# A vision block with tree feed-forward on one core: leaves of six trees gathered by indirect DMA instead of four

## The reference

```python
h = patches @ W.T + b                                # 768 -> 256
h = h + attn(layernorm(h))                           # gated attention, no softmax
h = h + ffn(layernorm(h))
# attn(x): xn = x / rms(x) * g;  u, v, base = split(silu(xn @ uv_w.T))   # 512, 512, 128
#   q, k = rope(base * gamma + beta);  kernel = relu((q k' + w_rel) / sqrt(128)) ** 2
#   return x * res_scale + (u * (kernel @ v)) @ o_w.T
# ffn(x): 8 trees of 255 nodes; logits = x @ W_in.T + b_in
#   from the root go right where logits > 0, seven times: 8 nodes visited per tree
#   return (silu(logits) * visited) @ W_out.T
```

## Time and profile before

| | |
|---|---|
| median of three runs | 2206.93 us |
| profiled execution | 2201.36 us, its span 2199.5 us |
| mean granted TensorE clock | 0.981 of 2.4 GHz |
| busy in the span: PE, VectorE, ScalarE, GpSimd | 94%, 74%, 63%, 35% |
| DMA queue of the indirect DMAs | 103.02 MB, 17.4% of the 16 engines |
| DMA queue of all others | 59.71 MB, 9.3% |

### The profile page before, as it was taken

How to read it: one execution, slowest core, us unless ns; L and a number is a source line. 1 busy time by engine, 2 the same in 40 slices (tenths; PEclk the granted TensorE clock), 3 DMA queues, 4 the chain that set the end, 5 groups by cost and what they waited for, 6 DMA issues and landing times.

```text
span 2199.5 us, 42461 instructions
## 1 busy us (share of the span) xinstructions
PE 2066.1 (94%) x13256; PEld 1941.8 (88%) x13256; DVE 1621.5 (74%) x4210; ACT 1395.2 (63%) x3085; POOL 774.1 (35%) x905
## 2 busy tenths in 40 slices
PE   6899999999999999999999999999999999999997
PEld 5789889899988898888998898988889988889887
DVE  5678777777777787777777777777777877777775
ACT  5556666666666566566666665666665666656654
POOL 2752333232333333332323333323323233333233
PEclk8999999999999999999999999999999999999999
DMA  5331322222322223222223222222223232222222
GB/s 146 85 94 52 89 73 66 73 76 63 83 71 65 81 55 84 75 64 73 77 62 84 70 73 73 64 75 77 65 70 84 55 85 69 73 73 66 63 67 74
DMA packets 81999, 163.13 MB, mean 74 GB/s; under 512 B 17102, under 2 KB 48048, under 8 KB 81968
## 3 DMA queue, kind: packets, MB, share of 16 engines
q0 software_dynamic: 40960, 103.02, 17.4%
q1 hardware_dynamic: 41008, 59.71, 9.3%
HBM read 148.76 MB, written 13.90 MB: 74 GB/s over the span
## 4 chain that ended last, share of the span: by engine, by line
PE 84%; another core or an unknown queue 5%; ACT 4%; POOL 3%; issue 2%; DVE 1%; DMA 1%; ACTq 0%; POOLq 0%; SPq 0%; DVEq 0%
PE front L1142 10%; PE front L1144 9%; PE front L1143 9%; PE hid_ps L1142 9%; PE hid_ps L1143 9%; PE hid_ps L1144 9%; PE out_acc L1142 6%; PE out_acc L1143 6%; PE out_acc L1144 6%; PE out_acc L1378 4%; PE front L1177 2%; PE front L1184 2%; PE hid_ps L1366 2%; PE hid_ps L1337 2%
## 5 line engine op out<-in xcount | busy, mean ns | idle before, releaser
L474 POOL DMA_INDIRECT leaf_rows<-leaf_table,leaf_at x512 | 532.4, 1040 | 163.9 <-issue 163.4
L453 POOL TENSOR_TENSOR inv_root<-to_root,minus_half 98x8 f32<-98x8 f32 x64 | 111.0, 1734 | 728.3 <-DVE to_root L885 404.6
L528 ACT ACTIVATE hid_hi<-hid 128x392 fp32r<-128x392 f32 (+1 forms) x256 | 177.8, 695 | 237.1 <-PE out_acc L1144 155.4
L1142 PE MATMUL out_acc<-hid_hi,outw_lo 128*128 128x392 f32 x768 | 293.4, 382 | 2.6 <-DVE hid_lo L835 2.3
L1142 PE MATMUL hid_ps<-ffn_x,in_lo 128*128 128x392 f32 x768 | 282.3, 368 | 6.2 <-POOL in_lo L445 5.8
L1143 PE MATMUL hid_ps<-ffn_x,in_hi 128*128 128x392 f32 x768 | 266.3, 347 | 0.0
L1144 PE MATMUL hid_ps<-ffn_x,in_hi 128*128 128x392 f32 x768 | 264.7, 345 | 0.0
L1144 PE MATMUL out_acc<-hid_hi,outw_hi 128*128 128x392 f32 x768 | 264.6, 345 | 0.0
L1143 PE MATMUL out_acc<-hid_lo,outw_hi 128*128 128x392 f32 x768 | 264.4, 344 | 0.0
L473 POOL TENSOR_TENSOR held<-minus_half 98x1 f32<-98x1 f32 x128 | 47.2, 369 | 489.9 <-issue 428.7
L718 ACT ACTIVATE leaf_rows<-leaf_rows,leaf_act 98x256 f32<-98x256 f32 x512 | 218.2, 508 | 0.1
(11 more groups left out here) (140 smaller groups left out, 5808.2 us busy)
## 6 DMA issues: line engine op xcount, KB each, us to landing
x_raw<-x SPq DMA_DIRECT2D x192, 196.0 KB, 2.4
out<-out_stage SPq DMA_DIRECT2D x32, 392.0 KB
leaf_rows<-leaf_table,leaf_at POOLq DMA_INDIRECT x512
leaf_table<-leaf_rows SPq DMA_DIRECT2D x4, 256.5 KB, 4.7
out_stage<-in_w SPq DMA_DIRECT2D x4, 256.0 KB
tok_major<-tok_w SPq DMA_DIRECT2D x3, 256.0 KB, 4.3
late_raw<-out_w SPq DMA_DIRECT2D x6, 128.0 KB
u<-uv_w SPq DMA_DIRECT2D x1, 576.0 KB, 4.2
```

Source lines behind the costliest of these rows:

```text
L453: pool.tensor_tensor(inv_root[:, 0:size], to_root[:, 0:size], minus_half[:, 0:size], ALU.pow).then_inc(roots_ok, 1)
L474: pool.indirect_dma_start(row_slot(s, g), None, table, bass.IndirectOffsetOnAxis(ap=leaf_at[:, s, g:g + 1], axis=0), element_offset=s * P ...
L528: act.activation(out, src, ACT.Copy).then_inc(done, 1)
L1142: pe.matmul(out, w[1], x_parts[0], start=start, stop=False)
```

## The change

Trees 0 to 5 are gathered and 6 and 7 dense; there are 12 row slots, so tree s takes the slots of tree s - 3. The slots of the hidden values get names but stay two. The rounds are cut elsewhere, and all five lists of calls are ordered anew. Core of the diff:

```diff
-GATHERED = 4
+GATHERED = 6
-ROW_SLOTS = 8
+HID_SLOTS, HID_HALVES = 2, 2
+ROW_SLOTS = 12
-LATE_SPLITS = (((0, 1), (2,), (3,), (4,), (5,)), ((6,), (7,), (8, 9), (10, 11), (12, 13)))
+LATE_SPLITS = (((0, 1), (2,), (3,), (4,), (5,)), ((6,), (7,), (8,), (9,), (10, 11)))
...
                     act.wait_ge(decided, TREES * i + t + 1)
-                if b == halves(t) - 1 and (t >= 2 or not first(i)):
-                    act.wait_ge(hid_lo_ok, TREES * i + t - 1)
+                if t >= HID_SLOTS or not first(i):
+                    act.wait_ge(hid_lo_ok, TREES * i + t - HID_SLOTS + 1)
```

More of the change, by code:

```diff
@@ L771, in body @@
                 silu_v(n, 2)
                 silu_v(n, 3)
-                v_high(n, 2)
[L774 to L783, removed]
+                x_high(nx, 2)
+                leaf_silu(i, 1)
+                qk_high(n, 0)
@@ L784, in body @@
+                leaf_number(i, 3)
+                silu_u(n, 0)
+                qk_high(n, 1)
+                scale_rows(i, 1)
+                silu_u(n, 1)
+                silu_tree(i, 5, 0)
+                leaf_silu(i, 2)
+                v_high(n, 2)
+                leaf_number(i, 4)
                 if first(n):
                     build_rows()
+                v_high(n, 3)
+                scale_rows(i, 2)
                 kern_high(n, 0)
+                hid_high(i, 4)
                 kern_high(n, 1)
@@ L1410, in body @@
-                mix(i, 2)
-                tree_visits(p, 6)
-                mix(i, 3)
-                tree_out(p, 3, 1)
-                tree_out(p, 4, 0)
-                project_o(i, 0, range(0, 3))
-                project_o(i, 0, range(3, EC))
-                project_o(i, 1, range(0, EC))
-                embed(n, 0)
-                turn_h(i, 1, 0)
-                turn_h(i, 1, 1)
-                tree_out(p, 4, 1)
-                embed(n, 1)
-                tree_logits(p, 7, 0)
-                tree_logits(p, 7, 1)
@@ new lines, in body @@
+                turn_normed(n, 0)
+                turn_normed(n, 1)
+                tree_visits(i, 3)
+                tree_out(i, 1, 0)
+                make_base(n)
+                find_leaf(i, 2)
+                tree_out(i, 1, 1)
+                make_v(n, 0)
+                make_v(n, 1)
+                tree_logits(i, 4, 0)
+                tree_logits(i, 5, 0)
+                make_v(n, 2)
+                tree_out(i, 2, 0)
+                tree_visits(i, 4)
+                find_leaf(i, 3)
@@ L1450, in body @@
+                tree_out(i, 2, 1)
+                make_v(n, 3)
+                add_rows(i, 0)
+                make_u(n, 0)
+                make_u(n, 1)
+                tree_logits(i, 6, 0)
+                tree_visits(i, 5)
+                find_leaf(i, 4)
+                scores(n, 0)
+                tree_out(i, 3, 0)
                 if first(n):
                     turn_rows()
-                tree_out(p, 7, 1)
-                tree_logits(i, 4, 0)
-                turn_xn(n, 0)
-                turn_xn(n, 1)
@@ L1471, in body @@
-                tree_out(i, 2, 0)
-                make_v(n, 3)
-                add_rows(i, 0)
-                tree_out(i, 2, 1)
+                tree_out(i, 3, 1)
+                scores(n, 1)
+                add_rows(i, 1)
+                tree_logits(i, 6, 1)
+                tree_logits(i, 7, 0)
+                find_leaf(i, 5)
+                make_u(n, 2)
+                make_u(n, 3)
+                add_rows(i, 2)
+                mix(n, 0)
+                tree_visits(i, 6)
+                mix(n, 1)
@@ new lines, in body @@
+                mix(n, 2)
+                mix(n, 3)
+                tree_logits(i, 7, 1)
+                tree_out(i, 4, 0)
+                tree_out(i, 4, 1)
+                project_o(n, 0, range(0, 3))
+                project_o(n, 0, range(3, EC))
+                project_o(n, 1, range(0, EC))
+                tree_out(i, 5, 0)
+                tree_out(i, 5, 1)
+                turn_h(n, 1, 0)
+                turn_h(n, 1, 1)
+                embed(nx, 0)
+                embed(nx, 1)
+                embed(nx, 2)
@@ new lines, in body @@
+                embed(nx, 3)
+                tree_visits(i, 7)
+                embed(nx, 4)
+                embed(nx, 5)
+                turn_ffn_x(n, 0)
+                turn_ffn_x(n, 1)
+                add_rows(i, 3)
+                add_rows(i, 4)
+                turn_h(nx, 0, 0)
+                turn_h(nx, 0, 1)
+                tree_logits(n, 0, 0)
+                tree_logits(n, 1, 0)
+                add_rows(i, 5)
+                tree_out(i, 6, 0)
+                tree_visits(n, 0)
@@ L1476, in _ @@
+                tree_out(i, 6, 1)
+                tree_out(i, 7, 0)
+                find_leaf(n, 0)
+                tree_visits(n, 1)
             body(None, None, None, 0)
```

226 lines of the change are left out of this document (95 added, 131 removed).

## The result

The changed kernel took 2434.03 us (median of 4, 2423.41 to 2445.64) against 2206.67 us of the kernel before beside it (4 runs, 2200.00 to 2209.72): ratio 1.104, 95% interval 1.096 to 1.111. Forecast were 2129 us and faster. Its profiled execution has a span of 2421.6 us against 2199.5.

What follows compares the result with a forecast made beforehand. PE's dense row of matmuls was taken to bound the kernel: 2201.4 us less 77 for PE's net saving, waits and ends unchanged, gives 2124, plus 5.6 from profiled run to median, 2129 us; range 2060 to 2190.

Steps and rivals of the forecast that it cites:

- I take it that the store's transfer is what makes hand-overs late: Base chain: the output store's transfer delays `silu_base` after `make_base`; PE waits 3.1 us a round in the kernel before.
- I keep it equal: PE's wait around `make_base` and `make_v` stays as before, 3.1 us a round, held within +-0.7 a round, 20 us.
- The first rival: Base chain: `silu_base` waits for eight fetches, PE waits 5.4 us instead of 3.1; +30 us, 2237; chance 0.12.
- In the round at 87 us fetches run and the hand-over is immediate: Evidence against fetches as cause: with fetches but no output store, `silu_base` starts 0.04 us after `make_base`'s last matmul ends.
- PE's net work, -2.42 a round: Two gathered trees save 2.14 us of matmuls each and add 0.93: net 1.21 a tree, 77 us over 32 units.
- First and last rounds: Start and end of the kernel: +3 us at the end, -3 at the start, together nothing.
- rows in time: Tree 5's rows land at 42.2 to 44.8 us of the round, some 2 us to spare before PE wants `h`.
- GpSimd's sum: GpSimd per round: six trees' fetches 33.5 us plus 7.5 other work, together 41 of 64.7 us, so it fits.
- `norm_roots`: GpSimd: `norm_roots(n,1)`, behind all 24 fetches, is wanted at 49.5 us and has 9 us to spare.
- ScalarE and VectorE hidden: ScalarE gains +1.1 us a tree, VectorE +1.0, reaching 45.5 and 52.3 of 64.7 us a round; neither binds.
- a PE wait above 5 us for `silu_base`: Sign that the forecast is wrong: PE waits over 5 us in the base chain, where 3.1 a round was expected.
- a granted clock clearly below 0.98: Sign that the forecast is wrong: PE's granted clock in a middle stretch falls clearly below 0.98.

Runs made afterwards that it cites:

- e13: The kernel before with its output store cut from 128 to 16 partitions: 2205.29 us, 1.002 of the kernel before at 2200.34 us.
- e12: The kernel before with two of each tree's four fetches left out after the first unit: 2078.84 us, 0.944 of the kernel before at 2200.34 us.
- e17: The kernel before with tree 1's four fetches held until the unit's base is there: 2099.61 us, 0.955 of the kernel before at 2200.69 us.
- e15: The changed kernel itself, measured again: 2358.81 us, 1.068 of the kernel before at 2200.34 us.
- e14: The changed kernel with two of each tree's four fetches left out after the first unit: 2038.15 us, 0.925 of the kernel before at 2200.34 us.
- e4: The kernel before with tree 1's four fetches held until silu_base of the round is done: 2064.34 us, 1.001 of the kernel before at 2063.08 us.
- e1: The changed kernel with its output store cut from 128 to 16 partitions: 2040.39 us, 0.989 of the kernel before at 2063.08 us.
- e3: The changed kernel with two of each tree's four fetches left out after the first unit: 2029.07 us, 0.984 of the kernel before at 2063.08 us.
- e8: The changed kernel with a longer small GpSimd operation ahead of each tree's fetches: 2239.84 us, 1.086 of the kernel before at 2062.98 us.
- e18: The changed kernel with fetched rows of 64 floats instead of 513 after the first unit: 2425.17 us, 1.102 of the kernel before at 2200.69 us.
- e16: The changed kernel with fetches of trees 1 and 5 held, a pause before tree 2's, tree 5's later work moved back: 2220.23 us, 1.009.
- e6: The changed kernel with tree 1's fetches held until the unit's base, tree 5's until its gates: 2395.82 us, 1.085 of the kernel before at 2207.26 us.
- e2: The changed kernel with fetched rows of 64 floats instead of 513 after the first unit: 2041.22 us, 0.990 of the kernel before at 2063.08 us.

## Why the prediction was wrong

- **The step that failed** is "I take it that the store's transfer is what makes hand-overs late", and with it "I keep it equal". e13 took seven eighths of the store away where the waits exist and changed nothing (1.002, waits of 65.9 us in the stretch). e12 and e17 left the store and took the train apart, and the waits went (7.8 and 13.6 us; 0.944 and 0.955). The step put the wait after at 3.1 us a round and +-0.7; it was 6.7. The first rival, at 0.12, had the mechanism.
- **Its counter-evidence was misread.** "In the round at 87 us fetches run and the hand-over is immediate": only five fetches stand in a row there, in one of the first rounds, and the hand-over comes 5.0 us behind the start of the first of them (82.26), against 11.6 in the earlier trace rows. So that row differs from the earlier trace rows by the train as well as by the store, and I read only the second. The sign that was there, 1.19 us from the eighth fetch's end to `silu_base`, stood in the rival and was the rule: 1.15 to 1.21 us in all 20 rounds from 500 to 1840 us.
- **The rival's size, 2237, was short too.** It counted the train under the base chain. The new list also put trees 4 and 5 back to back under `mix` and `gate`: 78.6 us of idle time, where the kernel before has 1.1. And it priced the low clock at 1.6 us a round. Between e15 and e14 the round differs by 9.9 us; e15's listed waits are 118.3 us in the stretch, 6.3 a round, and e14's 0.3, so about 3.9 is left for matmuls at half clock and small gaps.
- **PE's net work, -2.42 a round: the direction right.** Start to start in one round of e4 and e1, the 24 removed matmuls were 4.6 us, `add_rows` +1.7 and `find_leaf` +0.3: -2.6. But `tree_visits` took 0.7 more and `embed` some 0.5; why is not shown (the clock isn't it: 1.00 in e1's stretch from 1000 to 1500 us). The round gained 1.2 (e4 to e1) and 1.6 (e12 to e14).
- **First and last rounds, "together nothing": mis-sized.** The end cost 13.7 us more in the quick group and 22.3 in the first measurement. With half the fetches (e3) it cost 1.7, so it is the last unit's fetches that stand in PE's way.
- **Right:** rows in time ("so nothing, at neither end"), GpSimd's sum, `norm_roots`, ScalarE and VectorE hidden. How thin that cover is e8 shows: 7.2 us later cost 3.3 us of PE a round.
- The text had signs for its own failure, "a PE wait above 5 us for `silu_base`; or a granted clock clearly below 0.98". The second came as written (0.912). The first came one step earlier in the chain: 5.7 us ahead of `make_base`, for the residual, while PE waited hardly at all for `silu_base` (0.5 us in the stretch).

The Trainium skill (SBUF — State Buffer, Who interferes with whom) says that DMA never contends with a compute engine. The prediction set its own reading against that rule and was wrong: the store (e13) and the rows' bytes (e18) do nothing to the hand-overs, and there the traces agree with it. The rule doesn't name what does.

What stays open: why fetches in a row hold up the hand-overs of PE, by which path, and what makes a group quick or late. Results reach ScalarE late as well as VectorE, so a contention of VectorE with GpSimd doesn't explain it. Every edit that shortened a train also left fetches out or moved them away from the waiting chain, so how much is due to the length and how much to the place was not separated. Trains of four are enough for some of it: under them VectorE stood up to 1.3 us (after, `add_rel_bias`) and 1.97 us (e16, the residual) with no releaser named. The changed kernel itself was never run in a quick group: 0.989 there is that of two variants of it. And it took 2434 us in the first measurement but 2359 in two late groups.

## What to carry to other kernels

When a result reaches an idle engine late, look at what GpSimd issues just then, and time the lateness from the end of its train of indirect DMAs. Keep trains short, and away from chains that wait for PE's results: one wait that cut a train of eight in two was worth 4.5% here where the lateness exists, and cost nothing where it doesn't. But check what stands behind rows that come later for it: in e6 and e8 that cost 3.2 and 3.3 us a round. Before a row is taken as evidence against a rival, ask in how many ways it differs from the row beside it.

## What the runs showed of the hardware

- In the late groups, results of TensorE reached VectorE and ScalarE late while eight indirect DMAs stood back to back on GpSimd (each 98 rows of 2052 bytes, 0.97 us and a gap of 0.30): up to 5.7 us (after, `turn_normed` over at 977.96, taken at 983.65), until 1.0 to 1.5 us behind the last. Four in a row cost PE 0.65 (e17) to 1.4 us a round (e6, e16). Rows of 256 bytes did the same (e18). In the quick groups the same trains made nothing late (e1, e2).
- One and the same kernel took 2063 us in two groups and 2200 to 2207 us in the others. With half the fetches the two kinds are 20 us apart (2058.85 and 2078.84) instead of 137 to 144, so most of it is this lateness.
- With the waits TensorE's granted clock is lower: mean 0.931 (e15) against 0.987 (e14) with the same matmuls.
